# Graph layer, linear attention and experts on one core: another order for some weight pages, loads and splits

## The chip, the cores and the metric

The kernel runs on one core of a Trainium2 chip. Its time is the device time of one execution in microseconds (us), and of several executions the median is given. The engines are TensorE (PE; PEld is its weight load), VectorE (DVE), ScalarE (ACT), GpSimd (POOL) and SyncE (SP, which here issues transfers only). ACT issues transfers as well. Every engine runs its own list of instructions in the written order, and semaphores order one list against another.

## The reference

The input is 1250 tokens of 768 features and a list of 21,250 edges. What is computed, cut to what matters here:

```python
xn = layernorm(x)
# graph part: two attention layers over the edges, of 4 heads x 192 and 2 heads x 96
out2 = gat(gat(norm(xn), W1, 4, 192), W2, 2, 96)
graph = concat([xn, out2]) @ Wu + bu
# linear attention, then an MLP of 768 -> 3072 -> 768
q, k, v = split(ln1(xn) @ qkv_w + qkv_b)
q, k = elu(q) + 1, elu(k) + 1
y = (q @ (k.T @ v)) / (q @ k.sum()) @ proj_w + proj_b      # per head
m = xn + y
m = m + gelu(ln2(m) @ fc1_w + fc1_b) @ fc2_w + fc2_b
x = x + graph + m
# two of four experts, chosen from the mean over the tokens, and a last layer norm
return x + experts(layernorm(x))
```

A layer's softmax over edges is worked out densely: 1250 x 1250 edge counts are made by matmuls of one-hot rows, and `md` holds the logarithm of a count for each pair of tokens.

## The kernel before, in words

Tokens are cut into 10 tiles of 125 (`NT`, `TP`), features into 6 pieces of 128 (`KT`). A float32 product is made of three matmuls: both operands are split into a high half (written by ACT or POOL) and a low half (written by DVE or POOL), and high x high, high x low and low x high are added. A weight page is 128 rows of a matrix; it lands in one of three buffers (`raw`), is split, and its buffer is loaded anew when the low half is written (`bw_split`). All orders are written out by hand; nothing is planned.

The stages, by the profile's times:

- Edges, 0 to 235 us. Turn t of ten makes one-hot rows on DVE (`one_hots`, S1h and D1h) and counts edges with them on PE. Beside that each turn splits token tile t-2 (`x_low`, X_lo), the six Wu pages (`page_high` on ACT, `page_low` on DVE, in turns 0 and 2) and adds the graph product of tile t-4 to x (`graph_rows`: first bias, L1845, then PE's result, L1847). The sum goes to memory (wt_d) and the next tile of x comes in its place (xu), both by SP. After the last turn `gained_page` splits the six W1 pages, the last three of which SP loads (L453) ahead of the last stores of wt_d.
- First layer, 235 to 505 us: 40 steps, each with a softmax (ACT `sm`, L1468), transposes (PE L828) and a gather.
- Second layer, 505 to 630 us: 20 steps, two for each tile. Each step needs a tile of md, which ACT's queue brings. Each tile's graph rows are added in xw (DVE L2056) and stored in xg_d by SP (L564), and the next xw comes (L567). At the start of this layer SP issues four loads of normed tokens (xs, L549) and four broadcasts of bias rows (kvb, L557).
- Keys and values, 630 to 780 us, then queries to 869 us (18 jobs: PE L984, L999, L1010, L1013; DVE q_lo L2154, z_lo L2164). Beside the first queries POOL splits the six pages of the projection weight (wp, L1220 and L1221).
- Projection, 869 to 969 us, tile by tile: PE `project`, DVE adds xn and takes moments, ACT normalises (`normal`, xl, L1660), DVE adds the graph part (`residual`, L2211, in TK), PE turns the normed tile back to features (`tile_back`, L670), ACT copies it (`l_features`, ftl, L1667) and DVE splits it (`split_tile`, X_hi L2110 and X_lo L2111). SP brings xn and xg for each tile into three buffers (L582, L583), POOL adds the projection's bias to xn (`tile_bias`, L1305).
- Then the MLP and the experts to the end, over 1000 us of nearly unbroken matmuls that the change leaves as they are.

Of the kernel before, what the change touches and what calls it, by code (L numbers as in the profile page):

```python
# [14 lines left out]
P = 128  # L15
# [152 lines left out]
def gps_layer(nc, A, out):  # L168
    ctx = ExitStack()
    with ctx:  # L170
# [21 lines left out]
        follow("act_once", ("s_f", 1), ("e_ec", 1), ("v_cp", 1), ("at_r0", 1), ("xs_a", 4))  # L192
        for k in ("st", "ag", "rc", "sd", "rs", "xh"):
            follow(f"norm_{k}", (f"l_{k}", NT), (f"y_{k}", NT), (f"f_{k}", NT))
# [236 lines left out]
        def _(sp):  # L431
# [61 lines left out]
            for k in range(3, KT):  # L493
                rows_page(PG_W1 + k, A["gnn_W1"], k)
# [56 lines left out]
            sp.wait_ge(*at("at_o", STEPS1))  # L551
# [48 lines left out]
            for t in range(3 + GK, NT):  # L600
                tile_in(t)
# [51 lines left out]
        def _(pe):  # L653
# [517 lines left out]
        def _(pool):  # L1171
# [111 lines left out]
            for k in range(KT):  # L1283
                split_page(PG_PJ + k, wp[k])
# [17 lines left out]
            def tile_bias(t):  # L1302

                pool.wait_ge(*at(f"l_in{t % 3}", 32 * (t // 3 + 1)))
# [9 lines left out]
            for t in range(6, NT):  # L1314
# [17 lines left out]
        def _(act):  # L1332
# [3 lines left out]
            for k in range(3):  # L1336
# [6 lines left out]
               pb[0:TP, 1, 0:4 * EW].rearrange("p (v n) -> p v n", v=4)[:, :, 0:NEP], ACT.Copy).then_inc(sem("e_ec"), 1)  # L1343
            act.wait_ge(*at("v_tr", 1))
# [16 lines left out]
            def page_high(i, hi, **kw):  # L1361
                act.wait_ge(*at(f"bw_in{i % NRAW}", page_landed(i)))
                A_(hi[:], raw[i % NRAW][:], **kw).then_inc(sem("bw_hi"), 1)

            act.wait_ge(*at("v_cp", 1))
            act.wait_ge(*at("zsel_ok", 1))
# [9 lines left out]
            for k in range(3):  # L1376
                page_high(PG_WU + k, wu[k][0], func=ACT.Copy)
# [209 lines left out]
            for i in range(STEPS1, STEPS):  # L1587
# [6 lines left out]
                every(i - STEPS1, 8, H2, norm_scale)  # L1594
# [92 lines left out]
            for t in range(NT):  # L1687
                root("l", t, "eps8")
# [3 lines left out]
                else:  # L1692
                    for u in {3: (0, 1), 4: (2, 3)}.get(t, (t - 1,)):
                        l_features(u)
                if t >= 2:
                    act.wait_ge(*at("l_tr", t - 1))
                normal("l", t, RM[f"xl{t % 2}"][:], TK[:, t, :])
            l_features(NT - 1)
# [65 lines left out]
        def _(dve):  # L1764
# [76 lines left out]
            def graph_rows(u):  # L1841
# [3 lines left out]
                ch.link(v.tensor_tensor(xu[:], xu[:], RE["bu"][:], ALU.add))  # L1845
                dve.wait_ge(*at("wt_mm", u + 1))
# [19 lines left out]

            dve.wait_ge(*at("bnd", 1))
# [4 lines left out]
            for t in range(NT):  # L1872
                one_hots(t)
                if t >= XFIRST + 2:
                    graph_rows(t - XFIRST - 2)
                edges_of(t + 1)
                if ln_tiles(t):
                    token_norms(t)
                for k in {0: (0, 1, 2), 2: (3, 4, 5)}.get(t, ()):
                    page_low(PG_WU + k, wu[k])  # L1880
# [16 lines left out]
                for u in x_tiles(t):  # L1897
                    x_low(u)

# [13 lines left out]
            edge_table(NT - 1)  # L1913
            gained_page(0)
            gained_page(1)
            graph_rows(NT - 4)
            x_low(NT - 2)
            gained_page(2)
            graph_rows(NT - 3)
# [5 lines left out]
            gained_page(5)  # L1925
            graph_rows(NT - 2)
            graph_rows(NT - 1)
# [275 lines left out]
            def residual(t):  # L2203

                dve.wait_ge(*at("l_xh", t + 1))
                v.tensor_tensor(TK[:, t, :], TK[:, t, :], RM[f"xg{t % 3}"][:], ALU.add).then_inc(sem("l_tok"), 1)

            for t in range(NT):
# [13 lines left out]
                if t == 3:  # L2222
                    split_tile(0, RM["ftl0"][:], "l_ev", "l_x")
                    split_tile(1, RM["ftl1"][:], "l_ev", "l_x")
# [182 lines left out]
```

## Time and profile before

| | us |
|---|---|
| median of 3 runs | 1996.64 |
| lowest and highest | 1996.44, 1998.62 |
| profiled execution | 1996.43 |
| its span | 1994.7 |
| PE busy in it | 1912.6 (96%) |
| DVE busy | 1173.1 (59%) |
| ACT busy | 606.3 (30%) |
| POOL busy | 416.2 (21%) |

The span runs from the first to the last instruction that the profile shows. The granted clock is TensorE's, in parts of its full speed: 0.983 over the whole span. All other engines stand beside PE, so what counts is where PE waits and where it runs at the lower clock.

### The profile page before, as it was taken

The numbers are of one execution on the slowest core, as the hardware profiler recorded it, in microseconds if no ns is written. First come the engines' busy times: TensorE is split into PE (matmuls) and PEld (weight loads), VectorE is DVE, ScalarE is ACT, GpSimd is POOL, SyncE is SP. The second block draws the span as 40 slices with busy tenths as digits, with TensorE's granted clock in tenths as the row PEclk, the third lists the DMA queues.
The fourth block names the chain that finished last, engine by engine and source line by source line (L and its number), as shares of the span: only waits on it lengthen the run. The fifth ranks groups of instructions, "written<-read, shape, count | busy, mean of one in ns | idle before, by whom it ended". The sixth has DMA issues, their size and how long they took to land.

```text
span 1994.7 us, 28285 instructions
## 1 busy us (share of the span) xinstructions
PE 1912.6 (96%) x10979; PEld 1820.4 (91%) x10979; DVE 1173.1 (59%) x2085; ACT 606.3 (30%) x1175; POOL 416.2 (21%) x317
## 2 busy tenths in 40 slices
PE   7999899999799999998999999999989999999997
PEld 4677899999799999788999999999989999999997
DVE  7898669998795324666535344253557435274347
ACT  6533228887684311224301001010341001010013
POOL 1000001210001433113224134041115314043120
PEclk9999999999799999999999999999989999999999
DMA  4322401111223210013112011020232102021013
GB/s 146 118 101 96 136 7 55 51 42 53 113 103 128 71 48 17 8 66 114 49 47 64 13 52 49 15 64 15 66 93 64 37 28 64 9 79 38 27 52 119
DMA packets 76958, 125.50 MB, mean 63 GB/s; under 512 B 3350, under 2 KB 47672, under 8 KB 76830
## 3 DMA queue, kind: packets, MB, share of 16 engines
q1 hardware_dynamic: 74448, 115.09, 17.8%
q10 hardware_dynamic: 2382, 8.68, 1.1%
q8 instruction: 84, 1.38, 0.3%
q14 instruction: 44, 0.36, 0.1%
HBM read 98.30 MB, written 25.45 MB: 62 GB/s over the span
## 4 chain that ended last, share of the span: by engine, by line
PE 79%; DVE 7%; ACT 5%; issue 4%; DMA 3%; POOL 1%; DVEq 1%; ACTq 0%; SPq 0%; POOLq 0%
PE pb L1076 25%; PE pa L662 23%; PE pb L662 9%; PE pa L728 3%; PE pa L842 3%; PE pb L794 3%; PE pb L984 3%; PE pb L842 2%; PE pa L828 2%; DMA md<-md_d 1%; ACT sm L1468 1%; PE pb L873 1%; ACT o1h L1493 1%; PE pb L900 1%; DVE S1h L1820 1%
## 5 line engine op out<-in xcount | busy, mean ns | idle before, releaser
L1707 ACT ACTIVATE tr<-pb,V 128x418 f32<-128x418 f32 (+1 forms) x144 | 87.9, 610 | 770.0 <-PE pb L1076 770.0
L1076 PE MATMUL pb<-X_hi,uw_hi 128*128 128x416 f32 (+1 forms) x864 | 306.1, 354 | 3.2 <-DVE uw_lo L2297 3.2
L1076 PE MATMUL pb<-X_hi,uw_lo 128*128 128x416 f32 (+1 forms) x864 | 305.7, 354 | 0.0
L1076 PE MATMUL pb<-X_lo,uw_hi 128*128 128x416 f32 (+1 forms) x864 | 305.6, 354 | 0.0
L662 PE MATMUL pa<-dw_hi,hh 128*125 128x384 f32 x960 | 246.5, 338 | 0.7 <-ACT tr L1707 0.7
L662 PE MATMUL pa<-dw_hi,hl 128*125 128x384 f32 x960 | 245.9, 337 | 0.0
L662 PE MATMUL pa<-dw_lo,hh 128*125 128x384 f32 x960 | 245.9, 337 | 0.0
L2244 DVE CAST hh<-tr 128x418 fp32r<-128x418 f32 (+1 forms) x144 | 116.3, 808 | 207.8 <-ACT tr L1707 207.8
L1220 POOL CAST uw_hi<-raw 128x768 fp32r<-128x768 f32 x47 | 42.3, 899 | 700.6 <-PE pb L1076 608.7
L662 PEld LDWEIGHTS pa<-dw_hi,hh 128*125 128x125 f32 x960 | 172.3, 185 | 1.4 <-ACT tr L1707 1.0
L662 PEld LDWEIGHTS pa<-dw_lo,hh 128*125 128x125 f32 x960 | 172.9, 185 | 0.0
L662 PEld LDWEIGHTS pa<-dw_hi,hl 128*125 128x125 f32 x960 | 172.9, 185 | 0.0
L1076 PEld LDWEIGHTS pb<-X_hi,uw_hi 128*128 128x128 f32 x864 | 164.1, 190 | 5.6 <-issue 3.6
L1076 PEld LDWEIGHTS pb<-X_lo,uw_hi 128*128 128x128 f32 x864 | 164.2, 190 | 1.6
L1076 PEld LDWEIGHTS pb<-X_hi,uw_lo 128*128 128x128 f32 x864 | 163.5, 189 | 2.0
L2246 DVE TENSOR_TENSOR hl<-tr,hh 128x418 fp32r<-128x418 f32 (+1 forms) x144 | 150.8, 1047 | 5.0
L2258 DVE SCALAR_TENSOR_TENSOR TK<-pa,gate,TK 125x768 f32<-125x768 f32 x60 | 61.0, 1016 | 145.6 <-PE pa L662 145.6
L2256 DVE TENSOR_TENSOR TK<-pa,TK 125x768 f32<-125x768 f32 x50 | 47.9, 958 | 151.8 <-PE pa L662 151.8
L728 PE MATMUL pa<-S1h,D1h 125*125 125x418 bf16 x540 | 110.4, 358 | 4.7 <-DVE S1h L1820 4.7
L728 PEld LDWEIGHTS pa<-S1h,D1h 125*125 125x125 bf16 x540 | 65.4, 139 | 49.1 <-DVE S1h L1820 35.3
L1820 DVE TENSOR_SCALAR S1h<-iota,ec 125x1254 bf16<-125x1254 f16 x200 | 108.0, 540 | 0.0
L1221 POOL TENSOR_TENSOR dw_lo<-raw,dw_hi 128x768 fp32r<-128x768 f32 x48 | 99.4, 2071 | 3.8
(396 smaller groups left out, 3538.8 us busy)
## 6 DMA issues: line engine op xcount, KB each, us to landing
raw<-in_L_mix_fc_w SPq DMA_DIRECT2D x48, 384.0 KB, 3.3
raw<-in_L_ffn_w SPq DMA_DIRECT2D x47, 384.0 KB, 3.2
md<-md_d SPq DMA_DIRECT2D x11, 610.4 KB
md_d<-mds SPq DMA_DIRECT2D x10, 610.4 KB
md<-md_d ACTq DMA_DIRECT2D x8, 610.4 KB
raw<-in_L_mix_qkv_w SPq DMA_DIRECT2D x24, 192.0 KB, 4.2
TOK<-in_x SPq DMA_DIRECT2D x10, 375.0 KB
xn_d<-TOK SPq DMA_DIRECT2D x10, 375.0 KB
```

Source lines behind the costliest of these rows:

```text
L662: last = nc.tensor.matmul(slot[:, c, :], x_[:, cols], w_[:, c * HD2:(c + 1) * HD2], start=(k == 0 and n == 0), stop=(k == len(blocks) - 1 ...
L728: last = nc.tensor.matmul(acc[0:TP, c, 0:CH], RM[f"D1h{q}"][:], RM[f"S1h{q}"][:, c * CH:(c + 1) * CH], start=False, stop=True, skip_group_ ...
L794: last = nc.tensor.matmul(bank, x_[:, cols], w_[:, c * HD2:(c + 1) * HD2], start=(k == 0 and q == 0), stop=(k == KT - 1 and q == 2))
L842: last = nc.tensor.matmul(sums(i)[0:TP, 0:n], RX[f"PT{i % 2}"][:, columns(j)], rows, start=(j == 0), stop=(j == NT - 1))
L984: last = nc.tensor.matmul(pb[:, r % 2, 0:w], w_[:, m * P:(m + 1) * P], x_[:, o:o + w], start=(kk == 0 and n == 0), stop=(kk == KT - 1 and ...
L1076: last = nc.tensor.matmul(pb[:, j % 4, 0:n], w_[:, kk, :], x_[:, kk, o:o + n], start=(kk == 0 and q == 0), stop=(kk == KT - 1 and q == 2))
L1221: g_.tensor_tensor(lo, src, hi.bitcast(fp32), ALU.subtract).then_inc(sem("bw_split"), 1)
L1707: last = A_(RE[f"tr{j % 3}"][:, 0:w], pb[:, j % 4, 0:w], ACT.Identity if func == "mish" else func, bias=bias(b))
L1820: v.tensor_scalar(RM[f"S1h{q}"][:], RM["iota"][:], ec[:, ds(first + (q % 2) * EW, 1)], None, ALU.is_equal).then_inc(sem(f"oh{q}"), 1)
L2244: v.tensor_copy(hb_hi[b][:, o:o + w], z).then_inc(sem("h_hi"), 1)
L2246: v.tensor_tensor(hb_lo[b][:, o:o + w], z, hb_hi[b][:, o:o + w].bitcast(fp32), ALU.subtract).then_inc(sem("h_lo"), 1)
L2258: ins = v.scalar_tensor_tensor(out=w2(out_), in0=wide(pa, t % 2), scalar=scale, in1=w2(tok), op0=ALU.mult, op1=ALU.add, **kw)
```

## The change

Four places are altered.

Edges: ACT makes the high halves of Wu pages 0 to 2 before it copies V, DVE makes the low halves of pages 0 and 1 before the first one-hots, that of page 2 in turn 0, and those of pages 3 to 5 in turn 3 instead of 2. `graph_rows` is cut in two: the bias is added at the end of the turn before (`graph_bias`), so that only the addition of PE's result is left after the one-hots. After the last turn the order of rows, splits and pages is another, and W1's pages 3 to 5 are loaded by ACT's queue.

Second layer: the loads of xs0 to xs3 and kvb come one after each stored graph tile, and ACT's scaling of the first four normed tiles (`norm_scale`) starts at step 13 instead of 8.

Queries: POOL waits before each wp page for every second query job.

Projection: a tile is turned back to features two tiles later instead of one, DVE makes the scales before the split, xn is loaded as soon as the tile two before was added (l_x1 instead of l_tok), and xg has a semaphore and waits of its own; xg3 to xg9 go by ACT's queue.

The diff, cut to its core:

```diff
@@ SP, edges and second layer
-            for k in range(3, KT):
-                rows_page(PG_W1 + k, A["gnn_W1"], k)
...
             sp.wait_ge(*at("at_o", STEPS1))
-            for t in range(2):
-                xs_load(t)
-            for g in range(2):
...
-            for t in (2, 3):
-                xs_load(t)
             for t in range(NT):
...
+                if t < 4:
+                    xs_load(t)
+                elif t < 6:
+                    kvb_load(t - 4)
@@ SP, projection
             def tile_in(t):
                 if t >= 3:
-                    sp.wait_ge(*at("l_tok", t - 2))
+                    sp.wait_ge(*at("l_x1", t - 2))
                 sp.dma_start(RM[f"xn{t % 3}"][:], xn_d[t]).then_inc(sem(f"l_in{t % 3}"), 16)
-                sp.dma_start(RM[f"xg{t % 3}"][:], xg_d[t]).then_inc(sem(f"l_in{t % 3}"), 16)
...
-            for b in range(GK):
+            for b in range(3):
+                graph_in(b)
@@ PE
-                for u in {3: (0, 1), 4: (2, 3)}.get(t, (t - 1,)):
+                for u in {3: (0, 1)}.get(t, (t - 2,)):
                     tile_back(u)
...
                 if n == 0:
+                    tile_back(NT - 2)
+                if n == 1:
                     tile_back(NT - 1)
-                if n == 1:
                     pe.wait_ge(*at("l_ev", NT - 1))
@@ POOL
             for k in range(KT):
+                pool.wait_ge(*at("q_ap", 2 * k + 1))
                 split_page(PG_PJ + k, wp[k])
...
-            for t in range(3):
+            for t in range(4):
                 tile_bias(t)
             pool.wait_ge(*at("att", QJOBS))
             for b in range(3):
                 up_split(0, b)
-                tile_bias(3 + b)
+                tile_bias(4 + b)
@@ ACT
+            for k in range(3):
+                page_high(PG_WU + k, wu[k][0], func=ACT.Copy)
...
                 if k == 3:
                     x_out(NT - 1)
+                    for m in range(3, KT):
+                        i = PG_W1 + m
+                        act.wait_ge(*at("bw_split", i - NRAW + 1))
+                        act.dma_start(raw[i % NRAW][:], A["gnn_W1"][m * P:(m + 1) * P, :]).then_inc(sem(f"bw_in{i % NRAW}"), 16)
...
-                every(i - STEPS1, 8, H2, norm_scale)
+                every(i - STEPS1, 13, H2, norm_scale)
...
             for t in range(NT):
+                if t >= 3:
+                    act.wait_ge(*at("l_tok", t - 2))
+                    act.dma_start(RM[f"xg{t % 3}"][:], xg_d[t]).then_inc(sem(f"lg_in{t % 3}"), 16)
+                    for u in {3: (0, 1)}.get(t, (t - 2,)):
+                        l_features(u)
                 root("l", t, "eps8")
@@ DVE
+            for k in range(2):
+                page_low(PG_WU + k, wu[k])
...
                 one_hots(t)
                 if t >= XFIRST + 2:
                     graph_rows(t - XFIRST - 2)
+                for k in {0: (2,), 3: (3, 4, 5)}.get(t, ()):
+                    page_low(PG_WU + k, wu[k])
...
-                for k in {0: (0, 1, 2), 2: (3, 4, 5)}.get(t, ()):
-                    page_low(PG_WU + k, wu[k])
...
                 for u in x_tiles(t):
                     x_low(u)
+                if t >= XFIRST + 1:
+                    graph_bias(t - XFIRST - 1)
...
             def residual(t):
...
+                dve.wait_ge(*at(f"lg_in{t % 3}", 16 * (t // 3 + 1)))
...
-                if t >= 4:
-                    split_tile(t - 2, RM[f"ftl{t % 2}"][:], "l_ev", "l_x")
                 scales("l", t)
...
+                for u in () if t < 3 else (0, 1) if t == 3 else (t - 2,):
+                    split_tile(u, RM[f"ftl{u % 2}"][:], "l_ev", "l_x")
```

How instructions move, first DVE's list at the end of the edges, from the last `mds` of the turns on. Before (xu, bu is the bias of the graph rows, xu, pb or pa their addition, w1_lo a low half of W1):

```order
L1853 TENSOR_TENSOR mds1<-mds1,t0_1 125x1250 [waits e_ln]
L1906 TENSOR_SCALAR c0w<-raw0,V 128x768 [waits bw_hi]
L1864 SCALAR_TENSOR_TENSOR w1_lo0<-raw0,V,w1_hi0 128x768 [waits bw_hi]
L1909 SCALAR_TENSOR_TENSOR c0w<-raw1,V,c0w 128x768 [waits c0_w,bw_hi]
L1864 SCALAR_TENSOR_TENSOR w1_lo1<-raw1,V,w1_hi1 128x768 [waits bw_hi]
L1845 TENSOR_TENSOR xu0<-xu0,bu 125x768 [waits xu_in0]
L1847 TENSOR_TENSOR xu0<-pb,xu0 125x768 [waits pe_rows,dve_chain]
L1858 TENSOR_TENSOR X_lo<-fx,X_hi 128x6x125 [waits x_ev]
```

After:

```order
L1863 TENSOR_TENSOR xu0<-xu0,bu 125x768 [waits xu_in0]
L1875 TENSOR_TENSOR mds1<-mds1,t0_1 125x1250 [waits e_ln,dve_chain]
L1869 TENSOR_TENSOR xu0<-pb,xu0 125x768 [waits pe_rows]
L1880 TENSOR_TENSOR X_lo<-fx,X_hi 128x6x125 [waits x_ev]
L1932 TENSOR_SCALAR c0w<-raw0,V 128x768 [waits bw_hi]
L1886 SCALAR_TENSOR_TENSOR w1_lo0<-raw0,V,w1_hi0 128x768 [waits bw_hi]
L1935 SCALAR_TENSOR_TENSOR c0w<-raw1,V,c0w 128x768 [waits c0_w,bw_hi]
L1886 SCALAR_TENSOR_TENSOR w1_lo1<-raw1,V,w1_hi1 128x768 [waits bw_hi]
```

The bias of tile 6 stands ahead of `mds1`, and the addition and X_lo ahead of the first two pages of W1 instead of behind them.

SP's list at the start of the second layer. Before (xs are the normed tokens, kvb the bias rows, xw and xg_d the graph rows):

```order
L549 DMA xs0<-xn_d 125x768 [waits pe_sums]
L549 DMA xs1<-xn_d 125x768
L557 DMA kvb0<-in_L0_mix_qkv_b 125x384 x2
L557 DMA kvb1<-in_L0_mix_qkv_b 125x384 x2
L549 DMA xs2<-xn_d 125x768
L549 DMA xs3<-xn_d 125x768
L564 DMA xg_d<-xw0 125x768 [waits dve_rows]
L564 DMA xg_d<-xw1 125x768 [waits dve_rows]
L567 DMA xw0<-wt_d 125x768 [waits xg_out0]
L564 DMA xg_d<-xw2 125x768 [waits dve_rows]
L567 DMA xw1<-wt_d 125x768 [waits xg_out1]
L564 DMA xg_d<-xw0 125x768 [waits dve_rows]
```

After:

```order
L562 DMA xg_d<-xw0 125x768 [waits dve_rows,pe_sums]
L550 DMA xs0<-xn_d 125x768
L562 DMA xg_d<-xw1 125x768 [waits dve_rows]
L565 DMA xw0<-wt_d 125x768 [waits xg_out0]
L550 DMA xs1<-xn_d 125x768
L562 DMA xg_d<-xw2 125x768 [waits dve_rows]
L565 DMA xw1<-wt_d 125x768 [waits xg_out1]
L550 DMA xs2<-xn_d 125x768
L562 DMA xg_d<-xw0 125x768 [waits dve_rows]
L565 DMA xw2<-wt_d 125x768 [waits xg_out2]
L550 DMA xs3<-xn_d 125x768
L562 DMA xg_d<-xw1 125x768 [waits dve_rows]
```

The eight loads no longer stand ahead of the first store, but one by one behind the stores and the loads of xw.

ACT's list in the middle of the projection. Before (ftl is `l_features`, xl is `normal`, ve its root):

```order
L1656 ACTIVATE ve<-mv,V 125x1 [waits norm_ag]
L1667 ACTIVATE ftl0<-pb,V 128x125 [waits l_x,pe_side]
L1667 ACTIVATE ftl0<-pb,V 128x125 x5
L1660 ACTIVATE xl1<-TK,nm,rs 125x768 [waits norm_rs,pe_side]
```

After:

```order
L1705 DMA xg1<-xg_d 125x768 [waits l_tok]
L1682 ACTIVATE ftl0<-pb,V 128x125 [waits l_x,pe_side]
L1682 ACTIVATE ftl0<-pb,V 128x125 x5
L1671 ACTIVATE ve<-mv,V 125x1 [waits norm_ag]
L1675 ACTIVATE xl0<-TK,nm,rs 125x768 [waits norm_rs,pe_side]
```

The copy of features stands ahead of the root of the tile, belongs to the tile two before, and a load of xg has come in front of it, which waits for DVE's addition (l_tok).

## Rows read from the trace of the kernel before

**Rows 1.** The page, section 1 (engine, busy us, share, instructions) and section 4.

```profile
PE 1912.6 (96%) x10979; PEld 1820.4 (91%) x10979; DVE 1173.1 (59%) x2085; ACT 606.3 (30%) x1175; POOL 416.2 (21%) x317
...
PE 79%; DVE 7%; ACT 5%; issue 4%; DMA 3%; POOL 1%; DVEq 1%; ACTq 0%; SPq 0%; POOLq 0%
```

**Rows 2.** Waits of TensorE: engine, tile, line <- releaser: us in all, times, longest.

```profile
PE pa L670 <- ACT xl L1660: 5.2, 2, 3.2
PE pb L670 <- ACT xl L1660: 4.0, 1, 4.0
PE pb L783 <- DVE pr L1946: 3.7, 1, 3.7
...
PE pa L999 <- DVE q_lo L2154: 3.2, 3, 1.2
PE pb L662 <- DVE xu L1847: 3.0, 6, 0.5
...
PE pb L1013 <- DVE z_lo L2164: 2.1, 1, 2.1
```

**Rows 3.** Chain that ended last, end of the edges: start us, us, what.

```profile
213.21 9.71 DMA wt_d<-xu
222.93 8.83 DMA xu<-in_x
```

**Rows 4.** Busy time by stretch: PE, PEld, DVE, ACT, POOL, PEclk, DMA share, GB/s.

```profile
556.00:572.00 16.00, 14.99 (x121) 14.42 (x120) 14.69 (x25) 14.73 (x27) 0.00 (x0) 1.00 0.29 102
572.00:604.00 32.00, 30.34 (x250) 29.50 (x249) 30.01 (x52) 27.14 (x48) 0.00 (x0) 1.00 0.32 130
604.00:620.00 16.00, 15.49 (x123) 15.22 (x122) 8.83 (x20) 9.15 (x25) 0.00 (x0) 1.00 0.32 103
620.00:630.00 10.00, 9.80 (x59) 9.53 (x57) 3.16 (x5) 0.85 (x3) 0.00 (x0) 1.00 0.32 129
```

**Rows 5.** DMA issues from 500 to 640 us: tiles, queue, count, KB each.

```profile
xs<-xn_d SPq DMA_DIRECT2D x6, 375.0 KB
...
kvb<-in_L_mix_qkv_b SPq DMA_DIRECT2D x4, 187.5 KB
```

**Rows 6.** TensorE by time: start us, us, what, [idle before <- releaser].

```profile
542.48 1.83 PE L828 MATMUL pa<-ident,sm 125*125 125x125 f32 x7 [2.39 <-ACT sm L1468]
...
560.65 1.35 PE L828 MATMUL pa<-ident,sm 125*125 125x125 f32 x10 [0.50 <-ACT sm L1468]
```

**Rows 7.** Busy time by stretch, in which the granted clock (PEclk) is low.

```profile
540.00:550.00 10.00, 7.61 (x39) 7.52 (x39) 7.30 (x14) 6.88 (x14) 0.00 (x0) 0.66 0.19 68
810.00:815.00 5.00, 4.16 (x13) 3.73 (x14) 3.70 (x8) 0.52 (x1) 0.00 (x0) 0.66 0.01 2
926.00:931.00 5.00, 5.00 (x18) 5.00 (x19) 3.36 (x8) 3.40 (x8) 0.31 (x1) 0.50 0.34 134
965.00:970.00 5.00, 5.00 (x20) 4.81 (x19) 3.42 (x6) 4.11 (x8) 0.00 (x0) 0.66 0.00 0
```

**Rows 8.** SP by time, the first store of graph rows (xg_d) and the next.

```profile
556.05 9.87 SPq L564 DMA_DIRECT2D xg_d<-xw  x2
```

**Rows 9.** GpSimd, 780 to 815 us: count, busy us, mean ns, idle.

```profile
L1221 POOL TENSOR_TENSOR wp_lo<-raw,wp_hi 128x768 fp32r<-128x768 f32 x6 | 12.0, 1994 | 0.5
```

**Rows 10.** VectorE by time, the split of the queries.

```profile
801.30 2.10 DVE L2154 TENSOR_TENSOR q_lo<-qe,q_hi 128x418 fp32r<-128x418 f32 x1
...
806.51 0.59 DVE L2154 TENSOR_TENSOR q_lo<-qe,q_hi 128x416 fp32r<-128x416 f32 x1
```

**Rows 11.** Chain that ended last, in the projection.

```profile
905.17 1.81 POOL xn L1305
...
912.36 2.43 DVE X_lo L2111
...
921.11 3.70 ACT ftl L1667 x11
...
939.53 7.75 DMA xg<-xg_d
```

More of the change, by code:

```diff
@@ L192, in gps_layer @@
         follow("act_once", ("s_f", 1), ("e_ec", 1), ("v_cp", 1), ("at_r0", 1), ("xs_a", 4))
+        for q in range(3):
+            n = 16 * len(range(q, NT, 3))
+            follow(f"tile_in{q}", (f"xw_in{q}", n), (f"lg_in{q}", n))
         for k in ("st", "ag", "rc", "sd", "rs", "xh"):
@@ L549, in xs_load, with kvb_load @@
                 sp.dma_start(normed(t)[:], xn_d[t]).then_inc(sem(normed_in(t)[0]), 16)
-            sp.wait_ge(*at("at_o", STEPS1))
-            for t in range(2):
-                xs_load(t)
-            for g in range(2):
+            def kvb_load(g):
                 for v in range(2):
@@ L557, in _ @@
                     sp.dma_start(RT[f"kvb{g}"][:, v, :], A["mix_qkv_b"][o:o + HD2].partition_broadcast(TP)).then_inc(sem("kvb_in"), 16)
-            for t in (2, 3):
-                xs_load(t)
+            sp.wait_ge(*at("at_o", STEPS1))
             for t in range(NT):
@@ L580, in tile_in, with graph_in @@
                 if t >= 3:
-                    sp.wait_ge(*at("l_tok", t - 2))
+                    sp.wait_ge(*at("l_x1", t - 2))
                 sp.dma_start(RM[f"xn{t % 3}"][:], xn_d[t]).then_inc(sem(f"l_in{t % 3}"), 16)
-                sp.dma_start(RM[f"xg{t % 3}"][:], xg_d[t]).then_inc(sem(f"l_in{t % 3}"), 16)
+            def graph_in(t):
+                sp.dma_start(RM[f"xg{t % 3}"][:], xg_d[t]).then_inc(sem(f"lg_in{t % 3}"), 16)
             fc1 = A["mix_fc1_w"].rearrange("(k p) n -> p k n", p=P)
@@ L596, in _ @@
                 tile_in(t)
-            for b in range(GK):
+            for b in range(3):
+                graph_in(b)
                 block_page(up_page(0, b), fc1[:, :, b * P:(b + 1) * P])
                 tile_in(3 + b)
-            for t in range(3 + GK, NT):
+            block_page(up_page(0, 3), fc1[:, :, 3 * P:4 * P])
+            for t in range(6, NT):
                 tile_in(t)
@@ L1312, in _ @@
                 up_split(0, b)
-                tile_bias(3 + b)
-            for t in range(6, NT):
+                tile_bias(4 + b)
+            for t in range(7, NT):
                 tile_bias(t)
@@ L1343, in _, with page_high @@
                pb[0:TP, 1, 0:4 * EW].rearrange("p (v n) -> p v n", v=4)[:, :, 0:NEP], ACT.Copy).then_inc(sem("e_ec"), 1)
+            def page_high(i, hi, **kw):
+                act.wait_ge(*at(f"bw_in{i % NRAW}", page_landed(i)))
+                A_(hi[:], raw[i % NRAW][:], **kw).then_inc(sem("bw_hi"), 1)
+            act.wait_ge(*at("zsel_ok", 1))
+            for k in range(3):
+                page_high(PG_WU + k, wu[k][0], func=ACT.Copy)
             act.wait_ge(*at("v_tr", 1))
@@ L1374, in moments_of @@
                 A_(mv[:, u, 1:2], st[:, u, 0, 1:2], ACT.Copy, scale=1.0 / D).then_inc(sem("ln_mv"), 1)
-            for k in range(3):
-                page_high(PG_WU + k, wu[k][0], func=ACT.Copy)
             for u in range(2):
@@ L1691, in _ @@
                     z_out(QLAST + 2 * t + 1)
-                else:
-                    for u in {3: (0, 1), 4: (2, 3)}.get(t, (t - 1,)):
-                        l_features(u)
                 if t >= 2:
@@ L1697, in _ @@
                 normal("l", t, RM[f"xl{t % 2}"][:], TK[:, t, :])
+            l_features(NT - 2)
             l_features(NT - 1)
@@ L1839, in token_norms, with graph_bias @@
                                        op0=ALU.mult, op1=ALU.mult).then_inc(sem("ln_rs"), 1)
-            def graph_rows(u):
+            def graph_bias(u):
                 xu = RE[f"xu{u % 3}"]
@@ L1845, in graph_rows @@
                 ch.link(v.tensor_tensor(xu[:], xu[:], RE["bu"][:], ALU.add))
+            def graph_rows(u):
+                xu = RE[f"xu{u % 3}"]
                 dve.wait_ge(*at("wt_mm", u + 1))
@@ L1913, in _ @@
             edge_table(NT - 1)
+            graph_rows(NT - 4)
+            x_low(NT - 2)
             gained_page(0)
             gained_page(1)
-            graph_rows(NT - 4)
-            x_low(NT - 2)
+            graph_bias(NT - 3)
+            graph_rows(NT - 3)
             gained_page(2)
-            graph_rows(NT - 3)
             x_low(NT - 1)
@@ L1925, in _ @@
             gained_page(5)
+            graph_bias(NT - 2)
             graph_rows(NT - 2)
+            graph_bias(NT - 1)
             graph_rows(NT - 1)
```

9 lines of the change are left out of this document (1 added, 8 removed).

## The prediction

> **What bounds the kernel now.** The page comes first: TensorE is busy 1912.6 of 1994.7 us and holds 79% of the chain that ended last [rows 1]. No edit takes a matmul away, so at most the 82 us in which TensorE stands idle, and what it loses at a lower clock, can be won. The waits of TensorE say where: of the idle time, the rows that the change can reach are 5.2 + 4.0 us before the transposes of the projection (xl), 3.7 at the end of the edges (pr), 3.2 and 2.1 in the queries, 3.0 in six waits of half a microsecond for graph rows (xu) [rows 2], and 2.39 at one step of the second layer [rows 6]. Then the granted clock. It is 1.00 nearly everywhere, but after each longer wait TensorE runs some microseconds at 0.50, the lower of its two levels (1.2 against 2.4 GHz) [rows 7]. A stretch of n us with granted clock c has lost n(1-c): 3.4 us at 540, 1.7 at 810, 2.5 at 926 and 1.7 at 965. Last the chain and the windows with the DMA's share, which tell what the waits hang on.
>
> The profiled execution took 1996.43 us, 1.7 more than its span and 0.2 less than the median of the runs. I sum against it and add the 0.2 at the end.
>
> **Projection.** The waits for xl are three: two of together 5.2 us, the longer 3.2, and one of 4.0 between them in time [rows 2]. The chain shows what each hangs on [rows 11]. Before the first, POOL's bias on xn (905.17) had been queued behind a weight split, then DVE split a tile (X_lo, 2.43 us) before it made the scales. Before the second, ACT copied eleven pieces of features (3.70 us) for two tiles back before it normalised. Before the third, the load of xg took 7.75 us from 939.53, since it was issued only when the addition two tiles earlier was done, and POOL's bias came behind it. The change answers each: scales ahead of the split; transposes, copy and split belong to a tile two earlier, so PE has a projection in hand while xl is made; xn is loaded on l_x1, before the residual, and the bias waits for xn alone; one more bias stands ahead of the weight splits. So I take all of 9.2 us, and with them the slow clock behind the last two, 2.5 + 1.7 [rows 7]. Together -13.4. What is added: tile_back(8) and (9) now stand behind the first jobs of the MLP, and `l_ev` of tile 9 is awaited before job 2. A job is 18 matmuls, about 3.5 us, and the chain scale, normal, transposes, copy hides there; if it doesn't, some 5 us of wait come back. Behind ACT's new wait on l_tok its copies, roots and `normal` are queued, but l_tok of t-2 is done a tile earlier. Bounds: -14 (nothing remains) and -5 (only the 5.2 in the pa banks, or the 4.0 and a microsecond of clock).
>
> **Second layer.** Eight loads leave the boundary. xs0 to xs3 are 375.0 KB each, kvb 4 x 187.5 KB [rows 5]; at the 130 GB/s of the stretch 572 to 604 [rows 4] that is 4 x 2.95 + 4 x 1.48 = 17.7 us. What goes: md's load arrives in time at step 8, so the wait of 2.39 us at 542.48 falls to the 0.50 that other steps show [rows 6], and the slow clock behind it goes. I take -1.9 - 3.4 [rows 7] = -5.3. What comes: the loads now stand behind the first store of graph rows, which SP issued at 556 [rows 8]. From there on the 125-row transfers (md, xw, xg_d) run at a DMA share of 0.32 and not above, whatever else is going on: 130 GB/s from 572 to 604 and 129 from 620 to 630 [rows 4]. The path is full for all but (1 - 102/130) x 16 = 3.4 us of 556 to 572 and (1 - 103/130) x 16 = 3.3 us of 604 to 620. So 17.7 - 6.7 = 11.0 us of transfers have no room, and all that follows, the last xw and its store ahead of TensorE's 630 us, comes later by that. Net +5.7. The bounds: everything is absorbed (the queued transfers are less urgent than they look, since TensorE waits for md and xw only) and only the -5.3 stays; or nothing is absorbed (17.7), nothing is gained, and two late md tiles cost a slow clock of 3.4 each, as at 542: +24.5. I take the ledger's value, since the windows are full where the loads go.
>
> The Trainium skill has a rule for this share: by "DMA: Bandwidth & Descriptors" (section "Why a DMA increments its semaphore by 16 and not by 1"), a copy is spread over the largest number of engines up to 16 that divides its slowest dimension, always the lowest-numbered ones, which for 125 rows is five of sixteen, or 0.31. By that rule, the trace agrees with its 0.32, and it speaks against this part of the change, since moving a load to another moment or queue leaves the same five engines to do it. If instead the share were that of one queue, moving W1's pages and xg to ACT's queue would win a little, and the loads would be absorbed.
>
> `norm_scale` on ACT at odd steps from 13 costs its 0.9 us beside TensorE at another step, at worst half a microsecond; I count nothing.
>
> **Edges.** Six waits of 0.50 for xu [rows 2] go, since only the addition is left behind the one-hots; of their 3.0 us I count 2.0, since DVE itself bounds one turn and part of another. But the end of the stage is not set by TensorE. The chain there is a store of wt_d, 9.71 us from 213.21, and behind it the load of the last xu, 8.83 us, then the wait of 3.7 [rows 2, 3]. Both are transfers of 375.0 KB, 2.95 us each as above, that share the path with md's stores. Their store is issued some microseconds earlier now (addition ahead of two W1 pages), but the path was nearly full already, so the chain moves only with what precedes it. I take -2.2. Three page splits in turn 3, 2.7 us of DVE, have no wait there to hide in; if they surface, +1 in sum. The other end is -6.7: both waits go in full, 3.7 + 3.0. ACT's queue for W1's pages changes nothing where the pages' path is the same.
>
> **Queries.** POOL's six low halves take 12.0 us [rows 9], and beside them DVE's q_lo takes 2.10 us, against 0.59 after them [rows 10]. Spread over six pairs of jobs, one split meets one q_lo or another at most, and DVE has a pair's time to recover. So of the 3.2 us in three waits for q_lo the two shorter go, 2.0 in all, while the longest, 1.2, stands at the last query job and stays; of the 2.1 for z_lo I take the part over the 1.2, 0.9, as a wait of the same chain [rows 2]. Together -2.9. The last split falls beside the last query job, where the third wait is: half a late low half's excess, +0.7 (2.10 - 0.59 = 1.5 [rows 10], halved). So -2.2. Bounds: -4.5, if all of z_lo's wait goes with its slow clock of 1.7 [rows 7], and +1, if each spaced split holds DVE up by one q_lo.
>
> The Trainium skill, "SBUF — State Buffer", section "SBUF: two separate sides", says that VectorE and GpSimd share one pair of ports as an exclusive lock, held for the whole instruction. By that rule a spaced split still blocks once, for up to its 2 us, and twelve such blocks stay wherever they are put; by the row, a block costs 1.5 us and reaches TensorE only where two follow each other.
>
> **Sum.** -13.4 + 5.7 - 2.2 - 2.2 = -12.1, so 1984.3 for the profiled execution and 1984.5 as a median.
>
> **Rivals.**
> - The eight loads are absorbed. For it: TensorE's own work never waits for xs or kvb in the layer, and a load that is late there may simply wait. Against it: the full windows. Second layer -5.3 in place of +5.7, 11.0 less: 1973.5.
> - The edges give all their waits, 6.7 in place of 2.2: 1980.0. For it the store of wt_d that goes out earlier; against it the full path.
> - The projection's waits come back: xn and xg still share one path, with the fc1 pages beside it, and the last tiles' wait moves behind the first MLP jobs. The first two waits go (2.0 + 4.0), and the third, with both slow clocks, comes back there: -6.0 in place of -13.4, which makes 1991.9.
> - Slower: the loads of xs and kvb make md's loads late for the softmax. The place is steps 10 to 19 of the second layer, the price 24.5 in place of 5.7: 1984.5 + 18.8 = 2003.3. It decides once this part costs more than 5.7 + 12.1 = 17.8 us; for it speaks that md already comes late at 542 with the same loads ahead of it, against it that each store and load is issued singly and md has two buffers.
>
> **How the numbers follow.** A run can tell a change from none at about 0.2%, 4 us: faster is below 1992.6, slower above 2000.6. Chances: forecast 0.50, loads absorbed 0.25, edges in full 0.08, projection only half 0.11, slower 0.06. Of the fourth, 0.02 lies within 0.2%, of the slower case 0.01. So faster 0.92, same 0.03, slower 0.05. The range goes from the absorbed loads, 1973, to the half projection, 1992; beyond lie the slower case and the two gains together.
>
> **What would show it.** In the profile after: waits for xl gone and a granted clock of 1.00 through the projection (projection right); no wait over 1 us at step 8 of the second layer, but in its second half waits of TensorE for sm or of DVE for md or xw, about 11 us in all (ledger right), or none (absorbed); the q_lo rows at 2.1 still there but no wait behind them; at the end of the edges still a wait for pr of 2 us or more behind a load of xu (path full), or none. I am wrong if the second layer's DMA share rises above 0.32 with the loads in it, or if a wait for l_ev of several us stands at job 2 of the MLP.

## The result, and the profile after

| | before | after |
|---|---|---|
| median | 1996.44 (9 runs, 1991.28 to 1998.62) | 1990.34 (9 runs, 1988.34 to 1994.45) |
| ratio after/before | | 0.9974, 95% interval 0.9966 to 0.9983 |
| span of the profiled execution | 1994.7 | 1989.4 |

The change makes the kernel faster, by 0.26% or 5.2 us by the ratio and 5.3 by the spans. The forecast was 12.1, so 6.8 are missing. The first matmul of each stage cuts the span into pieces (in us; the second layer is counted from the projection of its features, at 499.47 before and 500.34 after):

| stage | before | after | difference | forecast |
|---|---|---|---|---|
| edges | 235.17 | 235.71 | +0.5 | -2.2 |
| first layer | 264.30 | 264.63 | +0.3 | 0 |
| second layer, keys and values | 273.37 | 280.03 | +6.7 | +5.7 |
| queries | 96.53 | 97.68 | +1.2 | -2.2 |
| projection and all behind it | 1125.33 | 1111.35 | -14.0 | -13.4 |

The waits of TensorE say the same in another way. Columns as in [rows 2]:

```profile
PE pa L736 <- DVE S1h L1838: 8.8, 5, 3.1
...
PE pb L908 <- DVE xw L2085: 6.2, 2, 3.6
PE pb L791 <- DVE pr L1975: 5.5, 1, 5.5
PE pa L1007 <- DVE q_lo L2183: 4.3, 2, 3.3
...
PE pb L1021 <- DVE z_lo L2193: 1.4, 1, 1.4
...
PE pb L670 <- DVE xw L2085: 1.0, 1, 1.0
```

The three waits for xl and the six of 0.5 for xu are no longer there. In their place stand 6.2 + 1.0 us for xw, pr has grown from 3.7 to 5.5 and q_lo from 3.2 to 4.3, while z_lo has fallen from 2.1 to 1.4. S1h, the one-hots, has 8.8 in five waits on this bank, where before it had

```profile
PE pa L728 <- DVE S1h L1820: 4.7, 3, 2.6
```

**Edges.** VectorE at the end of turn 4, then TensorE at turn 5:

```profile
99.56 0.93 DVE L1880 TENSOR_TENSOR X_lo<-fx,X_hi 128x750 fp32r<-128x750 f32 x1
102.52 0.96 DVE L1863 TENSOR_TENSOR xu<-xu,bu 125x768 f32<-125x768 f32 x1 [2.02 <-DMA xu<-in_x]
103.92 0.26 DVE L1836 TENSOR_SCALAR D1h<-iota,ec 125x125 bf16<-125x125 f16 x1 [0.45 <-DVE xu L1863]
```

```profile
104.69 7.57 PE L736 MATMUL pa<-S1h,D1h 125*125 125x418 bf16 x31 [3.06 <-DVE S1h L1838]
```

The bias of a graph row (L1863) now stands ahead of the next turn's one-hots, and with it stands its wait for the load of x, 2.02 us. TensorE waits 3.06 for what is queued behind it, as much as the six waits had taken. So SP's last store of md but one, which leads the full path at the end, leaves only 0.24 us sooner, before and then after:

```profile
196.40 0.25 SPq L488 DMA_DIRECT2D md_d<-mds  x1
```

```profile
196.16 0.25 SPq L491 DMA_DIRECT2D md_d<-mds  x1
```

At the end the chain of waits reads as [rows 3] did:

```profile
202.72 20.70 DMA wt_d<-xu
...
223.44 8.87 DMA xu<-in_x
```

The store of wt_d leaves 10.5 us sooner (202.72 against 213.21) and lands half a microsecond later: it took 20.7 us instead of 9.7. TensorE was done 1.3 us sooner (at 230.2, by its wait of 5.48 for pr at 235.71) and so waits longer for pr.

**Second layer.** Busy time by stretch, columns as in [rows 4]:

```profile
556.00:572.00 16.00, 15.35 (x132) 15.18 (x131) 15.25 (x28) 13.04 (x24) 0.00 (x0) 1.00 0.32 131
572.00:604.00 32.00, 26.01 (x188) 25.29 (x186) 23.49 (x40) 23.55 (x41) 0.00 (x0) 0.89 0.32 130
604.00:620.00 16.00, 15.32 (x122) 14.81 (x122) 6.80 (x16) 8.72 (x23) 0.00 (x0) 1.00 0.33 129
620.00:637.00 17.00, 14.15 (x66) 13.91 (x66) 5.75 (x9) 2.10 (x6) 0.00 (x0) 0.80 0.33 130
```

The two stretches that had room, at 102 and 103 GB/s, are now at 131 and 129, and the full stretch lasts 7 us longer, at the same rate and share. VectorE's waits for the loads of xw, before and after:

```profile
DVE xw L2056 <- DMA xw<-wt_d: 2.5, 1, 2.5
```

```profile
DVE xw L2085 <- DMA xw<-wt_d: 19.9, 4, 6.2
```

TensorE waits 3.60 and 2.56 of its 7.2 us for xw in the middle of the layer, at 595 and 622, and behind each of the two the clock falls: the granted clock of 0.89 and 0.80 in the rows above is a loss of 3.5 and 3.4 us. Before, it was 1.00 in all of these stretches.

md is no longer late at the eighth step. In the trace after, the transposes that waited 2.39 at 542.48 [rows 6] wait 0.77 at 540.32, and no slow clock follows. Counted from the start of the stage, the transposes of the next step (551.13 before, 546.01 after) come 6.0 us sooner than before, and the first matmul of keys and values (630.30 before, 637.58 after) comes 6.4 later.

**Queries.** POOL's last split, VectorE's last q_lo and TensorE's wait for it, then the stretches:

```profile
871.67 0.83 POOL L1229 CAST wp_hi<-raw 128x768 fp32r<-128x768 f32 x1 [7.92 <-PE pb L1021]
872.57 1.81 POOL L1230 TENSOR_TENSOR wp_lo<-raw,wp_hi 128x768 fp32r<-128x768 f32 x1
```

```profile
871.70 1.02 DVE L2182 CAST q_hi<-qe 128x416 fp32r<-128x416 f32 x1
872.76 2.07 DVE L2183 TENSOR_TENSOR q_lo<-qe,q_hi 128x416 fp32r<-128x416 f32 x1
```

```profile
874.88 0.52 PE L1007 MATMUL pa<-q_hi,kd_hi 128*12 128x416 f32 x1 [3.28 <-DVE q_lo L2183]
```

```profile
872.00:877.00 5.00, 2.12 (x6) 1.24 (x6) 4.90 (x6) 0.15 (x1) 2.30 (x2) 0.72 0.32 98
877.00:882.00 5.00, 5.00 (x18) 4.45 (x18) 4.93 (x4) 1.80 (x2) 1.83 (x1) 0.59 0.55 174
```

The wait is 3.28 us, where before it was 1.2 [rows 2], since q_lo took 2.07 us beside POOL and the cast ahead of it 1.02. Around and behind it the granted clock is 0.72 and then 0.59, a loss of 3.4 us in these ten, where the five microseconds from 870 had 0.71 before, a loss of 1.5.

**Projection.** From its first matmul to the MLP:

```profile
877.00:975.00 98.00, 97.90 (x546) 93.20 (x546) 76.59 (x122) 42.20 (x94) 29.03 (x16) 0.98 0.31 101
```

TensorE is busy 97.9 of 98 us, and what the granted clock of 0.98 leaves is lost in the first five microseconds, behind the last wait of the queries. Before, the stretches at 926 and 965 alone had lost 4.2 us to the clock [rows 7].

### The profile page after: what moved, and what is told of

Read it like the earlier page. It is cut to its first block, busy times and chain, and to the rows that moved or that the text cites. A ratio compares the mean times of both kernels' runs of the same rounds, so it can differ in the third digit from the quotient of the medians.

```text
span 1989.4 us, 28296 instructions
## 1 busy us (share of the span) xinstructions
PE 1910.3 (96%) x10979; PEld 1820.2 (91%) x10979; DVE 1179.5 (59%) x2085; ACT 606.8 (31%) x1175; POOL 415.9 (21%) x317
## 4 chain that ended last, share of the span: by engine, by line
PE 79%; DMA 7%; DVE 5%; ACT 4%; issue 2%; SPq 1%; ACTq 0%; POOL 0%; DVEq 0%; POOLq 0%
PE pb L1084 25%; PE pa L670 24%; PE pb L670 9%; PE pa L736 3%; PE pa L850 3%; PE pb L802 3%; PE pb L992 3%; PE pa L836 2%; DMA xg_d<-xw 2%; PE pb L850 2%; DMA xw<-wt_d 2%; DMA xu<-in_x 1%; DMA wt_d<-xu 1%; DMA md_d<-mds 1%; ACT sm L1483 1%
```

## The experiments

Each kernel below was profiled once and timed. A stage's length in one profile is not exact: where no edit touches it, it scattered by 0.6 us in the edges (235.2 to 235.8), 1.5 in the first layer (264.3 to 265.8 in the ten kernels whose edges keep their transfers whole, 262.8 to 262.9 in the four in which they are cut), 5 in the second layer with keys and values (270.4 to 275.5), 1.4 in the queries (95.1 to 96.5) and 4.8 in the tail behind the first down matmul (989.1 to 993.9). Much of this is the clock: the same wait is followed by slow microseconds in one execution and not in another. At the late md of the second layer the ten microseconds from 540 have a granted clock of 0.66 in the trace before, 0.83 in those of pA, pE and Eord and 1.00 in that of C2. Whole spans scatter with all of these. So I go by stages, and by means over the kernels that share an edit. In the table "2nd" is the second layer with keys and values, "proj" runs from the first projection to the first down matmul. The last column compares a kernel's runs with runs of the kernel before that were timed beside them, with a 95% interval.

| kernel | edges | 2nd | queries | proj | span | ratio to before |
|---|---|---|---|---|---|---|
| before | 235.2 | 273.4 | 96.5 | 134.2 | 1994.7 | 1 |
| after | 235.7 | 280.0 | 97.7 | 120.5 | 1989.4 | 0.9974 |
| pA, edges part alone | 234.6 | 275.5 | 95.1 | 133.9 | 1997.5 | 1.0003 (0.9990 to 1.0016) |
| pC, second layer alone | 235.8 | 280.0 | 96.5 | 132.8 | 1998.8 | 1.0035 (1.0021 to 1.0050) |
| pD, wp pages alone | 235.6 | 274.6 | 97.7 | 134.1 | 2000.4 | 1.0001 (0.9990 to 1.0013) |
| pE, projection alone | 235.4 | 273.8 | 96.5 | 119.4 | 1979.5 | 0.9937 (0.9920 to 0.9954) |
| Eord, its order alone | 235.3 | 270.4 | 96.5 | 122.0 | 1982.0 | 0.9949 (0.9933 to 0.9966) |
| S2 | 236.0 | 266.0 | 97.7 | 120.8 | 1975.3 | 0.9901 (0.9885 to 0.9918) |
| C2 | 236.5 | 271.2 | 97.8 | 122.2 | 1982.3 | 0.9945 (0.9929 to 0.9962) |
| D2 | 234.6 | 279.3 | 92.2 | 121.0 | 1983.3 | 0.9944 (0.9928 to 0.9961) |
| SE | 226.8 | 279.6 | 96.1 | 121.0 | 1978.8 | 0.9918 (0.9903 to 0.9933) |
| bS | 230.9 | 266.6 | 96.5 | 129.8 | 1975.9 | 0.9919 (0.9899 to 0.9938) |
| best | 226.1 | 264.7 | 96.9 | 119.4 | 1960.6 | 0.9833 (0.9820 to 0.9846) |
| bestnoC | 226.6 | 266.3 | 92.2 | 120.9 | 1959.2 | 0.9833 (0.9817 to 0.9849) |

**The four parts one by one.** Each takes the part's lines of the diff above and leaves the other three as before.

> The kernel before with the edges part alone. Theory (parts add up, each stage as in the trace after): the wait of the bias for its load of x, 2 us, now stands ahead of turn 5's one-hots and TensorE waits 3.1 us there; the end of the edges does not move; in all +0.9 us against before (+0.5 by the start of the first layer). Rival (the forecast): -2.2 us, the six waits of 0.5 go and nothing takes their place.

> The kernel before with the second-layer part alone. Theory: the eight loads put 17.7 us of transfers into a path that is full from 556 us on; the second layer is 6.4 us longer, no other stage moves, in all +6.4. Rival (absorbed, the loss in the trace after came from the stage's other start): 0 to -5.

> The kernel before with the spaced projection pages alone. Theory: the short waits for q_lo go, but the last page's split falls on the last query job, whose wait is 3.3 us instead of 1.2, with a slow clock behind it; queries and that job 1.2 us longer. Rival (the forecast): -2.2 us.

> The kernel before with the projection part alone. Theory: all three waits for xl and the slow clock behind them go, -14 us. Rival: some of it hangs on the other parts (xg stored later, pages split later), -9 to -12.

The parts add up: -0.0063 + 0.0035 + 0.0001 + 0.0003 = -0.0024, against -0.0026 for all. Each ratio is sure only to 0.0012 to 0.0017, so the small ones, pA and pD, are told by their stages and not by their times. The second layer costs 6 to 7 us wherever the part is in (280.0, 280.0, 279.3, 279.6 against 270.4 to 275.5), the queries 1.2 by means (97.7 to 97.8 in four traces and 96.1 in one with the part, 95.1 to 96.5 without), the projection wins 12 to 15 (119.4 to 122.2 with the part, 132.8 to 134.2 without). The edges part wins nothing by means. What decides its size is in pA's own trace:

```profile
104.39 7.79 PE L726 MATMUL pa<-S1h,D1h 125*125 125x418 bf16 x37 [0.85 <-DVE S1h L1823]
...
234.61 0.75 PE L781 MATMUL pb<-ident,S 125*125 125x125 f32 x2 [5.10 <-DVE pr L1960]
```

```profile
201.90 20.43 DMA wt_d<-xu
222.35 8.86 DMA xu<-in_x
```

Here the wait at turn 5 is 0.85 us, not 3.1, and the whole end comes 1.1 us sooner than in the trace after: store, load and all. Five traces have the part with whole transfers in the edges, and they line up (in us):

| kernel | wait at turn 5 | last store of md but one leaves | edges end | between the two |
|---|---|---|---|---|
| pA | 0.85 | 195.25 | 234.61 | 39.4 |
| D2 | 1.28 | 195.17 | 234.62 | 39.5 |
| after | 3.06 | 196.16 | 235.71 | 39.6 |
| S2 | 3.60 | 196.58 | 236.01 | 39.4 |
| C2 | 3.84 | 196.91 | 236.47 | 39.6 |
| before | none | 196.40 | 235.17 | 38.8 |

So the end does move with what precedes the stores, and that hangs on the wait at turn 5, whose size changes from one execution to another with the landing of a load. The stretch behind that store is 0.6 to 0.8 us longer than before in all five; in the other four kernels without the part it is 38.7 to 38.8, too. Why stays open.

**What limits the second layer.** S2 is the changed kernel with

```diff
+        def rows_dma(eng, to, frm, name):
+            for a, b in ((0, TP - 5), (TP - 5, TP)):
+                eng.dma_start(to[a:b], frm[a:b]).then_inc(sem(name), 16)
...
-                sp.dma_start(xg_d[t], RW[f"xw{t % 3}"][:]).then_inc(sem(f"xg_out{t % 3}"), 16)
+                rows_dma(sp, xg_d[t], RW[f"xw{t % 3}"][:], f"xg_out{t % 3}")
```

and so for the transfers of md, xw, xg and xs, with the waits' counts doubled.

> The changed kernel, with each 125-row transfer of md, xw, xg and xs cut into one of 120 rows and one of 5. Theory (these transfers run on a few of the 16 DMA engines, which are full from 556 to 637 us): the 120 rows spread over more, the DMA share there rises above 0.33, the waits of TensorE for xw (7.2 us) and the late half's waits go, and the second layer with keys and values ends some 11 us sooner than in the changed kernel. Rival (the limit is the queue or memory, not the number of engines): share and rate stay at 0.32 and 130 GB/s, within 1 us of the changed kernel.

```profile
556.00:572.00 16.00, 15.37 (x127) 14.72 (x126) 15.19 (x28) 13.06 (x25) 0.00 (x0) 1.00 0.67 168
572.00:604.00 32.00, 29.49 (x242) 28.97 (x242) 28.85 (x49) 28.37 (x51) 0.00 (x0) 1.00 0.66 171
```

From 572 to 604 us the share of the DMA engines is 0.66 where it was 0.32, the rate 171 GB/s where it was 130. No wait of TensorE for xw is over 0.5 us, and the second layer with keys and values is 14.0 us shorter than in the changed kernel, where I had expected some 11, and 7 shorter than in the kernel before. The rival, share and rate unchanged, is out: neither the queue nor the memory held the rate at 130. What is left is the number of engines on which 125 rows run. The Trainium skill ("DMA: Bandwidth & Descriptors", section "Why a DMA increments its semaphore by 16 and not by 1") gives that number as the largest up to 16 that divides the rows, 5 for 125 and 15 for 120. By that rule the trace agrees: 5 of 16 is 0.31, the full stretch had 0.32, and 0.66 with the cut needs more than ten. No run cuts the rows so that the number of engines stays at five, so the share is the evidence here, and the part that two transfers in place of one may have in it is not measured by itself.

C2 keeps transfers whole and moves the eight loads into the first steps, where the path had room:

```diff
+            for n, (load, u) in enumerate(((xs_load, 0), (xs_load, 1), (kvb_load, 0), (kvb_load, 1), (xs_load, 2), (xs_load, 3))):
+                sp.wait_ge(*at("at_o", STEPS1 + 1 + n))
+                load(u)
...
-                if t < 4:
-                    xs_load(t)
-                elif t < 6:
-                    kvb_load(t - 4)
```

> The changed kernel, with the six loads xs0, xs1, kvb0, kvb1, xs2, xs3 issued one after each of the first six steps of the second layer, where the path moves only 41 to 79 GB/s, instead of behind the stores. Theory (ledger): 17.7 us of transfers leave the full stretch, so the layer is 11 us shorter than in the changed kernel, and md still comes in time. Rival: the loads make md late again as before the change, and only 5 to 6 us are won.

Second layer 271.2 against 280.0, so -8.9: between the theory and the rival. The path and TensorE's rows show why it is not the whole:

```profile
530.00:556.00 26.00, 22.68 (x195) 21.93 (x193) 22.86 (x39) 21.13 (x38) 0.00 (x0) 1.00 0.33 130
```

```profile
544.41 1.35 PE L834 MATMUL pa<-ident,sm 125*125 125x125 f32 x10 [2.39 <-ACT sm L1481]
...
573.58 1.36 PE L834 MATMUL pa<-ident,sm 125*125 125x125 f32 x10 [1.49 <-ACT sm L1481]
```

The loads fill the path up to 556, and md is late at the eighth step again, by the same 2.39 us. Of the three places tried, boundary, first steps or behind the stores, none was free and the last was the dearest. That the first steps are better than the boundary isn't shown: 271.2 lies within the 270.4 to 275.5 of the kernels with the loads at the boundary.

**Queries.** D2 is the changed kernel with one line other:

```diff
-                pool.wait_ge(*at("q_ap", 2 * k + 1))
+                pool.wait_ge(*at("q_ap", 2 * k))
```

> The changed kernel, with POOL waiting for query job 2k before wp page k, not 2k+1. Theory (the last split falls on the last query job's q_lo): the wait of 3.3 us there falls to about 1.2 and its slow clock goes, queries 2.5 to 3.5 us shorter. Rival (any spaced split costs the same somewhere): no change, another wait of 1 to 3 us at another job.

```profile
847.02 0.45 PE L1021 MATMUL pb<-z_hi,zsel 12*128 12x416 f32 x1 [0.57 <-DVE z_lo L2193]
...
870.11 0.36 PE L1007 MATMUL pa<-q_hi,kd_hi 128*12 128x416 f32 x1 [1.16 <-DVE q_lo L2183]
```

The last wait is back at 1.16 us, the slow clock behind it is back at the size that it had before (0.66 from 871 to 876, a loss of 1.7, most of it already in the projection), and the queries take 92.2 us: 5.5 less than in the changed kernel, where I had expected 2.5 to 3.5, and 4.3 less than before. Not all of it is the shift. Both kernels wait 1.42 us for z_lo at 814, but only one is slow behind it, the changed kernel first and then D2:

```profile
810.00:822.00 12.00, 10.58 (x46) 8.89 (x45) 9.35 (x13) 2.73 (x5) 2.89 (x2) 0.86 0.11 33
```

```profile
810.00:822.00 12.00, 10.58 (x53) 8.74 (x52) 9.29 (x14) 3.26 (x6) 1.48 (x2) 1.00 0.00 0
```

That is 1.7 us of the 5.5. SE, which has the part unshifted, isn't slow there either and takes 96.1, so 3.9 are left for the shift. Nor is the shift firm. In "best" below the same line is in, and there a split falls on z_lo:

```profile
822.67 0.71 PE L1027 MATMUL pb<-z_hi,zsel 12*128 12x416 f32 x1 [2.26 <-DVE z_lo L2199]
```

2.26 us and a slow clock, 96.9 in all. In "bestnoC" it doesn't (0.57 us for z_lo, and 92.2 in all).

**Projection.** Eord takes only the order of PE, ACT and DVE, with loads and biases as before.

> The kernel before with only the order of the projection changed (a tile turned back to features two tiles later, scales ahead of the split); loads, their waits and POOL's biases as before. Theory: the first two waits for xl (2.0 and 4.0) hung on the order and go with the clock behind them, the third (3.2 us) hung on the late load of xg and stays: about -9 of the -14. Rival: the order alone gives all, -14; or, since a load waits for the addition as before, it gives under -5.

```profile
953.22 0.86 PE L670 MATMUL pa<-ident,xl 125*128 125x125 f32 x6 [1.37 <-ACT xl L1661]
955.30 0.46 PE L1076 MATMUL pb<-X_hi,uw_hi 128*128 128x418 f32 x1 [1.22 <-ACT ftl L1668]
```

From projection to the first down matmul 122.0, so 12.2 of the 14.8 us of pE; I had expected 9. The order alone brings most; the third wait shrinks from 3.2 to 1.4, with 1.2 behind it at the first MLP job. These two waits are the 2.6 us to pE's 119.4, in which neither stands, and so what loads and biases bring.

**The edges' path.** SE is the changed kernel with the cut into 120 and 5 rows for wt_d, xu and md_d of the edges.

> The changed kernel, with the 125-row stores and loads of the edges (wt_d, xu, md_d) cut into 120 rows and 5. Theory (the end of the edges is set by the same full path, and turn 5 by the bias's wait for its load): the wait of 5.5 us for pr falls under 1, that of 3.1 us at turn 5 (about 105 us) too, and the edges end 5 to 8 us sooner. Rival (DVE's three page splits in turn 3, or the W1 pages, bind): the wait at turn 5 stays, and the end moves by less than 2 us.

The wait for pr is gone from the list of TensorE's waits, and so is that of turn 5; the edges take 226.8 us, 8.9 less, a little more than expected. The last store of md but one leaves at 193.50, so 2.7 of the 8.9 were won ahead of the stores, and 6.2 behind them. It also settles the rival: DVE's three page splits in turn 3 are still there, and TensorE waits no more than 0.47 us behind them, at turn 4.

**Together.** "best" has the cut for all these transfers, C2's place of the loads and D2's line. "bestnoC" has the cut and D2's line, with the second layer's loads as before the change. "bS" is the kernel before with nothing but the cut.

> The changed kernel with all 125-row transfers of md, wt, xu, xw, xg, xs, xn cut into 120 rows and 5, the xs and kvb loads one after each of the first six steps of the second layer, and POOL's wp pages one query job earlier. Theory (the three costs are independent): -14 in the second layer and keys and values, -5.5 in the queries, -6 in the edges against the changed kernel: a span of 1964, 1965 in all. Rival: TensorE's or DVE's own work binds once the transfers are fast, and only 20 of the 25 us come: 1970.

> As the kernel before this one, but with xs and kvb loaded at the boundary and norm_scale at step 8, as before the change. Theory (with the path no longer full it does not matter where the eight loads stand): within 1 us of it in the second layer. Rival: the loads still delay md at 536 to 542 us, and it is 3 to 6 us longer.

> The kernel before, its order untouched, with only the 125-row transfers cut into 120 rows and 5. Theory (full transfer path at the end of the edges and in the second layer; the projection's waits for xl are a matter of order): the wait for pr (3.7) goes, edges -3 to -5, second layer with keys and values -8 to -10 (what the path full of loads cost before), of the projection only the third wait, -3; in all -15 to -18, 1979. Rival (the path costs nothing before, only the change made it full): under -5.

best: median 1961.71 us against 1995.18, 33 us or 1.7% faster than before, and 28 faster than the change alone. That is 3 less than the 1965 expected, though the queries brought next to nothing of their 5.5: the edges and the second layer brought more (-9.6 and -15.3 against the changed kernel). bestnoC is the same (1960.98): once the path isn't full, it does not matter where the eight loads stand. Its second layer is 1.5 us longer in the one profile, less than the scatter, and md is in time at every step. bS: 1978.24 against 1994.15, 16 us from the cut alone. Edges -4.2, as expected; second layer -6.8, less than the 8 to 10 expected; projection -4.4, more than the 3 expected. But waits for xl stay, of the first all, of the second and third more than half (2.0, 4.0 and 3.2 before):

```profile
902.19 0.86 PE L678 MATMUL pa<-ident,xl 125*128 125x125 f32 x6 [2.04 <-ACT xl L1668]
912.25 1.51 PE L678 MATMUL pb<-ident,xl 125*128 125x125 f32 x6 [2.90 <-ACT xl L1668]
...
948.27 0.86 PE L678 MATMUL pa<-ident,xl 125*128 125x125 f32 x6 [1.74 <-ACT xl L1668]
```

What is left of them is a matter of order, and the cut doesn't reach it.

## Why the prediction was wrong, step by step

The direction was right and the four parts were the right ones; the size was not. Of the 6.8 us that are missing, 3.1 lie in the edges with the first layer (-2.2 to +0.9), 3.4 in the queries (-2.2 to +1.2), 1.0 in the second layer, and 0.6 go the other way in the projection.

- **Projection, right**: -13.4 and -14.0 measured. All three waits for xl and the slow clock went. The second slow stretch was under-read: over the ten microseconds from 923 the granted clock before was 0.66, a loss of 3.4 and not 2.5. And VectorE's split of 2.43 us (at 912.36) does not stand ahead of the first wait: the scales were done at 910.76. What xl stood behind there was the late bias and ScalarE's twelve copies, up to 913.65; the split delays the next tile's addition and so the second wait. That each wait hung on another edit was only half right: the order alone also took most of the third, which I had put down to xg's load.
- **Second layer, right in mechanism and nearly in size, the size partly by luck**: +5.7 and +6.7 (6.2 by means). The ledger of bytes against a full path foretold it: no room after 556, rate unchanged, waits for xw in the second half. Up to the ninth step 6.0 us were won, where I had 5.3, and behind it 12.4 lost, where I had 11.0. But the waits for xw are only 7.2; the slow clock behind two of them, 6.9, makes up for what they lack, and the ledger had no term for it. (Together they are 14.1; where 1.7 of it comes back I have not followed.) S2 shows that the path is the limit, C2 that the same loads elsewhere cost less.
- **Edges, wrong**: the step that failed is the term "of their 3.0 us I count 2.0", and with it the -2.2 (the sum has 0.2 more than the term, without a source). The six waits went, but the edges did not become shorter (means 235.5 with the part and 235.5 without). The bias took its wait for a load ahead of the one-hots, a wait of 2.02 us in the trace after that I had not priced, though the change's own rows show the bias moved; TensorE lost 3.06 at turn 5, and ahead of the last store of md but one only 0.2 us was won in place of 2.0. In pA and D2, where that wait was 0.85 and 1.28, it was 1.2. In SE, where there is none, it was 2.9: what I had counted was there to be won, had nothing taken its place. That the chain "moves only with what precedes it" held, but for 0.6 to 0.8 us by which the stretch behind that store grew, a cost that I had at nothing and whose cause stays open. The larger part of SE's 8.9, 6.2 us, lies in that full path, out of reach of any order.
- **Queries, wrong**: the term "+0.7" for the last split beside the last job. I had halved one late low half. It cost 2.1 us of wait (3.28 for 1.16) and a longer slow clock. The waits at the other jobs fell by 1.8, from 4.2 to 2.4, where I had taken 2.9. D2 moves every split by one job and wins 5.5, of which 1.7 is a slow stretch that SE's trace lacks without the shift. (The outer bound is wrong by its own terms, too: 2.0, all of z_lo's 2.1 and its slow clock of 1.7, less 0.7, make -5.1 and not -4.5.) The Trainium skill, "SBUF — State Buffer", section "SBUF: two separate sides", has VectorE and GpSimd lock the shared ports for a whole instruction. By that rule a spaced split still blocks once, and the trace agrees: POOL's split ends at 874.38, and VectorE's q_lo, begun at 872.76, at 874.83, 2.07 us for the 0.59 that it takes alone [rows 10].
- None of the rivals came about. The loads were not absorbed, the edges gave none of their waits instead of all, the projection's waits did not come back, and the slower case had no part in it.

## What to carry to other kernels

Before moving a load in time, sum the bytes of the stretch it comes into against the rate that the stretch already reaches: if they don't fit, the load costs its own length. Look at the DMA share at that rate, too: in the second layer it stood at 0.32 of 16 engines with the path full, the shape of the transfers was the limit, and cutting 125 rows into 120 and 5 won three times what the reordering did (16 us and 5). When an operation is moved ahead of another, its wait moves with it, and when splits are spaced out, the one that falls beside the last job has nothing behind which to hide. And before believing a stage's gain from one profile, look at the granted clock in it.

## What the hardware showed that I had not expected

- Twice the share of DMA engines gave 1.3 times the rate: 0.66 and 171 GB/s against 0.32 and 130 in 572 to 604 us. So, for the time that they were busy, the engines moved fewer bytes each. Why stays open; no run here tells it.
- One job's distance in a wait of POOL's was worth 3.9 to 5.5 us of TensorE in D2, and the same line gave next to none of it in "best": the wait for z_lo was 0.57 us in one and 2.26 in the other, with a granted clock of 1.00 and 0.83 in the 20 us around it.
- The same wait does not always cost the same clock. Behind the late md the ten microseconds from 540 were granted 0.66 in the trace before and 1.00 in C2's, though the wait was 2.39 us and TensorE busy 7.61 us of the ten in both.
- Parts of the program that no edit touches scatter by more than some edits are worth: the tail behind the first down matmul by 4.8 us of 991 from one execution to another. In the 20 runs of the kernel before beside pA, the fastest, 1990.93 us, had a mean granted clock of 0.985 and the slowest, 2000.98, one of 0.981, which is 8 of the 10 us between them.
